# A text and image-prompt attention kernel: first maxima's remainder in PSUM, loads moved ahead, a score chunk ahead of the ip products

## What is computed

```python
q = heads(x @ W_q); k_t = heads(text @ W_k); v_t = heads(text @ W_v)
probs_t = softmax(q k_t^T * 0.25)                 # 112 x 371 per head
text_out = probs_t v_t
k_ip, v_ip = heads(ip @ W_k_ip), heads(ip @ W_v_ip)
qsem = l2norm(probs_t text)                       # 112 x 512 per head
sem = qsem l2norm(ip)^T                           # 112 x 4
probs_ip = softmax(q k_ip^T * 0.25 + 0.5 * sem) * mask
out = (text_out + probs_ip v_ip) @ W_out + b_out + x
```

## Time and profile before

| | |
|---|---|
| median of 3 runs | 394.98 us (394.34, 394.98, 399.27) |
| the profiled execution's own time | 399.06 us, span 396.9 us, 9414 instructions |
| PE (TensorE products) | 381.2 us busy, 96% of the span, x3596 |
| VectorE, ScalarE, GpSimd | 221.2, 206.1, 208.2 us busy |
| chain that ended last | PE 77%, DVE 7%, DMA 6%, ACT 3%, POOL 3%, issue 2% |
| DMA | 37.87 MB in 29328 packets, mean 95 GB/s |
| granted TensorE clock | mean 0.993 of full |

### The profile page before, as it was taken

How to read it: one execution, slowest core, us unless ns; L and a number is a source line. 1 busy time by engine, 2 the same in 40 slices (tenths; PEclk the granted TensorE clock), 3 DMA queues, 4 the chain that set the end, 5 groups by cost and what they waited for, 6 DMA issues and landing times.

```text
span 396.9 us, 9414 instructions
## 1 busy us (share of the span) xinstructions
PE 381.2 (96%) x3596; PEld 319.6 (81%) x3596; DVE 221.2 (56%) x493; ACT 206.1 (52%) x483; POOL 208.2 (52%) x229
## 2 busy tenths in 40 slices
PE   8999996999999999999999999999999999999984
PEld 5658896877888888888989888888888888887773
DVE  0798482476367634665466545664466546644434
ACT  1533132665746564645457464656455466458722
POOL 7010280184527962586428652796258532944972
PEclk9999999899999999999999999999999999999998
DMA  8869989248204802273207620580207310001010
GB/s 268 264 158 222 166 214 181 46 154 155 72 0 155 151 13 58 79 163 66 85 7 196 102 67 19 154 151 13 75 0 161 66 41 3 2 9 34 2 31 15
DMA packets 29328, 37.87 MB, mean 95 GB/s; under 512 B 14346, under 2 KB 26619, under 8 KB 28603
## 3 DMA queue, kind: packets, MB, share of 16 engines
q1 hardware_dynamic: 28388, 36.22, 38.9%
q10 hardware_dynamic: 896, 1.07, 0.9%
HBM read 28.36 MB, written 8.81 MB: 94 GB/s over the span
## 4 chain that ended last, share of the span: by engine, by line
PE 77%; DVE 7%; DMA 6%; ACT 3%; POOL 3%; issue 2%; SPq 1%; ACTq 0%; DVEq 0%; POOLq 0%
PE PR L1000 38%; PE Y L1000 24%; PE O L1000 8%; PE P L1000 6%; DMA et<-ctxT 4%; DVE mx L889 2%; DMA qst<-ma 2%; POOL pb L598 1%; ACT big L750 1%; PE PR L1173 1%; POOL t L625 1%; ACT eh L683 1%; PE PR L1110 1%; DVE kst L841 0%; DVE kst L843 0%
## 5 line engine op out<-in xcount | busy, mean ns | idle before, releaser
L598 POOL TENSOR_TENSOR pb<-pb 128x448 f32<-128x448 f32 x78 | 89.1, 1143 | 102.5 <-DVE pb L911 97.0
L889 DVE TENSOR_REDUCE mx<-PR 112x1 f32<-112x371 f32 x160 | 82.2, 536 | 78.4 <-PE PR L1000 78.0
L1000 PE MATMUL Y<-er,Gh 128*128 128x448 f32 x240 | 95.1, 396 | 1.5 <-ACT er L754 1.3
L911 DVE TENSOR_TENSOR pb<-big,Y 128x448 f32<-128x448 f32 x120 | 72.6, 620 | 36.9 <-PE Y L1000 35.3
L1000 PE MATMUL Y<-er,Gl 128*128 128x448 f32 x240 | 87.2, 363 | 0.0
L750 ACT ACTIVATE big<-P 128x448 f32<-128x448 f32 x120 | 65.1, 542 | 25.5 <-PE P L1000 25.2
L754 ACT ACTIVATE er<-big 128x448 fp32r<-128x448 f32 x120 | 69.4, 578 | 3.8
L1000 PEld LDWEIGHTS Y<-er,Gh 128*128 128x128 f32 x240 | 45.1, 188 | 12.5 <-DVE pb L911 8.2
L1000 PE MATMUL PR<-kst,qst 96*112 96x371 bf16 x160 | 50.4, 328 | 0.6 <-DVE mx L889 0.5
L1000 PEld LDWEIGHTS Y<-er,Gl 128*128 128x128 f32 x240 | 45.2, 188 | 2.2
L1000 PE MATMUL P<-qst,kst 99*128 99x112 bf16 x480 | 41.9, 213 | 3.8 <-DMA qst<-ma 3.7
(11 more groups left out here) (177 smaller groups left out, 668.4 us busy)
## 6 DMA issues: line engine op xcount, KB each, us to landing
et<-ctxT SPq DMA_DIRECT2D x8, 752.0 KB, 4.3
kst<-kd SPq DMA_DIRECT2D x7, 720.0 KB, 7.3
kd<-ks SPq DMA_DIRECT2D x16, 288.0 KB, 2.8
qst<-qd SPq DMA_DIRECT2D x48, 70.0 KB, 2.3
kst<-kd SPq DMA_DIRECT2D x7, 480.0 KB, 9.8
kst<-kd SPq DMA_DIRECT2D x9, 240.0 KB, 9.2
qd<-kst SPq DMA_DIRECT2D x4, 336.0 KB, 5.9
vx<-xr SPq DMA_DIRECT2D x8, 140.0 KB, 2.6
```

The costliest lines, as they stand in the source:

```text
L598: pool.tensor_tensor(total, total, (pz, pm)[j], ALU.add).then_inc(s_S, 1)
L889: dve.tensor_reduce(mx[b % 2][:, h:h + 1], bank[0:S, 0:T], AX.X, ALU.max).then_inc(s_free[seq[u] % NR], 1)
L911: dve.tensor_tensor((pz, pm, pa[g % 2])[j], eb[g % 3][:, 448 * j:448 * j + 448], Y[y % 2][:, 0:448], ALU.mult).then_inc(s_P, 1)
L1000: return pe.matmul(o, st, mv, start=start, stop=stop, **kw)
```

## The change

Five edits. The remainder of the maxima's split, `mr`, is no longer a tile in SBUF but lies in a free part of the transpose's own PSUM bank (columns 128 to 239), so the last operation reads one operand from PSUM, waits for the one before it (`link`), and it, not the third, frees the bank. `load_e(1)` goes ahead of the kd writes of batch 0. `load_q(1)` goes ahead of the wait for the kd writes of batch 1 and of the k(1) load. The halves of context 1's split go between G(0,0), G(0,1) and G(0,2) instead of ahead of all three. And the word lists: in batch 0 one maximum moves from the fourth round to the third and one ahead of that round's gram products, in batches 1 to 6 the next group's first score chunk goes ahead of `cT`, and in the last batch's second round `pw` goes behind the gram products.

```diff
-          "p E g2 g1 pT g0 cT S0 S1 v o S2")
+          "p E g2 g1 pT g0 S0 cT S1 v o S2")
 EARLY = ("m S1- m S2- K1 S0 m g m S1 m S2 K2 m",
          "S0 m g m S1 m S2 v m m wo C",
-         "S0 m g m S1 m v S2 m V1",
-         "Kr S0 m g m m S1 m m v mT S2 GV",
+         "S0 m g m S1 m v S2 m V1 m",
+         "Kr S0 m g m S1 m m v mT S2 GV",
          "E g S0 v S1 S2")
-LATE = "p g2 g1 pT g0 cT S0 S1 v S2 o"
+LATE = "p g2 g1 pT g0 S0 cT S1 v S2 o"
-        "S0 r0 g2 pw S1 g1 g0 S2 v",
+        "S0 r0 g2 S1 g1 g0 pw S2 v",
...
-    order += [("K", 0, c) for c in range(3)] + [("Kr", 0), ("w", 1)] + qs[1] + [("kip", c) for c in range(3)] + [("vip",)] + split(1)
-    order += [("G", 0, i) for i in range(3)] + [("K", 1, c) for c in range(3)] + [("Kr", 1)]
+    order += [("K", 0, c) for c in range(3)] + [("Kr", 0), ("w", 1)] + qs[1] + [("kip", c) for c in range(3)] + [("vip",)]
+    order += [("G", 0, 0)] + split(1)[:2] + [("G", 0, 1)] + split(1)[2:] + [("G", 0, 2)] + [("K", 1, c) for c in range(3)] + [("Kr", 1)]
...
                 if u[0] == "K" and u[1] == 0:
                     c = u[2]
+                    if c == 0:
+                        load_e(1)
                     sp.wait_ge(s_k0s, c + 1)
...
-                    else:
-                        load_e(1)
...
                         load_q(0)
+                    if b == 1:
+                        q_written(sp)
+                        load_q(1)
                     sp.wait_ge(s_kw, written(b + 1))
...
-                    if b == 1:
-                        q_written(sp)
...
-                    if b == 1:
-                        load_q(1)
...
-                    p = bank[0:H, 0:S]
+                    p, mr = bank[0:H, 0:S], bank[0:H, 128:128 + S]
                     link(dve.tensor_scalar(ma[:, 0, :], p, -1.0, None, ALU.mult))
                     dve.scalar_tensor_tensor(ma[:, 1, :], p, -1.0, ma[:, 0, :], ALU.mult, ALU.subtract)
-                    dve.scalar_tensor_tensor(mr[:, :], p, -1.0, ma[:, 0, :], ALU.mult, ALU.subtract).then_inc(s_free[seq[u] % NR], 1)
+                    link(dve.scalar_tensor_tensor(mr, p, -1.0, ma[:, 0, :], ALU.mult, ALU.subtract))
+                    dve.tensor_tensor(ma[:, 2, :], mr, ma[:, 1, :], ALU.subtract).then_inc(s_free[seq[u] % NR], 1)
                     freed(dve, seq[u])
-                    dve.tensor_tensor(ma[:, 2, :], mr[:, :], ma[:, 1, :], ALU.subtract).then_inc(s_ms, 1)
+                    dve.sem_inc(s_ms, 1)
```

More of the change, by code:

```diff
@@ L225, in build @@
         ma = sb("ma", [H, 3, S], bf16)
-        mr = sb("mr", [H, S])
         OT = [sb(f"OT{i}", [128, NG, S]) for i in range(2)]
```

## The result

The changed kernel takes 394.02 us (median of 22 runs, 392.97 to 396.79), the kernel before 395.93 us beside it (22 runs, 394.34 to 400.69): ratio 0.9948, 95% interval 0.9929 to 0.9968, a gain of 1.9 us. The time lies inside the range (389.0 to 394.3) and 2.6 us above the point.

The account below looks back on a forecast made before the run. TensorE was taken to bound the kernel from 75 to about 360 us, with one large hole at the prologue's end. Terms 5.1 + 0.45 + 0.4 - 0.3 = 5.65 us, 3.6 taken from the 394.98 median: 391.4, range 389.0 to 394.3.

Parts of the forecast that it names:

- The step from the profiled execution to the median: Whole kernel: median 4.1 us below the profiled execution, so 1.55 to 5.65 left to gain; middle 3.6 taken.
- (a): Prologue, split of the maxima: remainder in PSUM cuts the slow last operation, `ma` ready 1.1 us sooner; bounds 0 and 1.15.
- (b): Prologue, SyncE's queue: q(1) issued in a DMA pause ahead of k(1), out of `ma`'s way; 2 us, bounds 0 and 2.3.
- (c): Prologue loads: context 1 ahead of the first `kd` writes brings k(1) 1.5 us sooner; bounds 0 and 2.
- (d): Prologue, K(1,0): G(0,0) ahead of the context's split frees its bank in time; 0.3 us, bounds 0 and 0.44.
- Start and clock: End of the prologue: first score chunk 3.8 us sooner, and 1.3 us from a clock that doesn't fall; together 5.1.
- (e): Batch 0: a maximum one round earlier removes a wait before the transpose; 0.45 us, bounds 0 and 0.5.
- (f): Six batches: S0 ahead of cT fills TensorE's wait, 0.1 us each; net 0.4 us, bounds -0.3 and 0.7.
- (g): Last batch: the power behind the sums turns TensorE's wait into a later one; cost 0.3 us, bounds -0.5 and 0.5.
- The stall isn't in ordinary runs: Rival, prologue: (a) to (c) shorten what was short, 0.85 us left; 394.1 us, chance 0.17.
- `ma` still waits in the queue: Rival, prologue: k(1) not sooner, `ma` lands near 67 and the clock still falls; 393.2 us, chance 0.22.
- The slower one: Rival, first maximum: context 1 delays the `kd`(0) writes and k(0), so TensorE waits; 396.7 us, chance 0.06.

Follow-up runs that it names:

- aa_before: The kernel before, unchanged, measured again: median 396.65 us, 0.8 below the kernel before in its group; its profiled execution took 395.74 us.
- ma_act: The kernel before with the three `ma` writes of batch 0 issued by ScalarE instead of SyncE: 6.2 us slower than before, six runs.
- no_a: The changed kernel with the remainder of the maxima back in SBUF: 394.62 us, 2.1 below the kernel before.
- the profiled pair: The profiled executions of the kernel before and of the changed kernel: 399.06 against 395.17 us.
- only_b: The kernel before with only q(1) loaded ahead of k(1): 396.65 us, 1.6 below the kernel before.
- only_a: The kernel before with only the remainder of the maxima in PSUM: 397.85 us, 0.4 below the kernel before.
- only_c: The kernel before with only context 1 loaded ahead of the kd writes of batch 0: 396.54 us, 1.7 below the kernel before.
- only_d: The kernel before with only G(0,0) ahead of the split of context 1: 399.14 us, 0.9 above the kernel before.
- no_c: The changed kernel with context 1 back behind the kd writes of batch 0: 395.32 us, 1.4 below the kernel before.
- no_b: The changed kernel with q(1) back behind k(1): 396.42 us, 0.3 below the kernel before.
- after_again: The changed kernel, unchanged, measured again: 394.81 us, 2.4 below the kernel before.
- before_again: The kernel before, unchanged, measured once more: 396.81 us, 0.4 below the kernel before; its profiled execution took 399.6 us.
- rest_efg: The kernel before with the word-list edits alone: 397.16 us, 0.3 below the kernel before; its profiled execution took 402.34 us.
- early_again: The changed kernel with the last batch's power in its old place and each `ma` write issued when its piece is ready: 393.91 us, 3.3 below before.

## Why the prediction was off, point by point

- **The step from the profiled execution to the median** failed: "I take the middle, 3.6". It treated the 4.1 us between the profiled execution and the median as one quantity of which half might be gained. Executions are of two kinds, and the median of the first measurement is of the short one: in aa_before, which stands for it, wait 0.53 us and full clock. The three times shown (394.34, 394.98, 399.27) already had two near 395 and one like the profiled 399.06. Read so, the long wait and its clock drop of the earlier trace rows had to be left out of the sum for a median almost whole. The prediction had that case at the end of its own scale ("the median has 1.55 left to gain"), and the runs gained 1.9. Of 2.6 us of error 1.7 is this; the other 0.95 is that the median of 22 runs of before is 395.93, not 394.98.
- **(a)** The duration came out (0.263 us in the median of all eight batches). The 1.42 us stand in nine traces that keep `mr` in SBUF, and end 0.12 to 0.13 us behind `El` in each; in the ten with `mr` in PSUM the operation takes 0.26 with `El` running beside it. One more trace tells it from the other side: in ma_act's execution at the low clock TensorE's transpose came so late that `El` (84.05, 3.50 us) was over, and the unchanged operation with both inputs in SBUF took 0.263 us in batch 0. `ma` is issued 1.42 us behind the transpose instead of 2.51: 1.1 sooner, as forecast. The rule of the Trainium skill (SBUF — State Buffer, the section on the ports), that such an operation waits for GpSimd's whole instruction, agrees with all of these. In time (a) showed no worth. Where TensorE waited for `ma`, k(1)'s end and not readiness set the landing; in no_a, where k(1) ended early (5.0 us behind the transpose), the late issue rather set it (`ma`'s last packet ended 1.3 us behind k(1)'s, in after 0.3), and TensorE had other work until then.
- **(b)** Forecast 2 us (0 to 2.3), measured 2.4 between the profiled pair (from k(1)'s last packet to the chunk 4.3, then 1.9), 2.1 to 3.4 over all traces. This edit by itself leaves no long runs (only_b: none of 12 above 398 us, where only_a has 5, only_c 3 and only_d 7). Of 121 runs with it in all kernels one is above 398, in no_c. The other edits together may do the same: no_b has none of 12, at a median 1.8 above no_a's. The ring-order rule of the Trainium skill (DMA: Bandwidth & Descriptors, queues, rings and completion order) isn't contradicted: wherever all of k(1) stood ahead of `ma` on SyncE's queue, the last `ma` packet ended behind k(1)'s last (64.70 against 64.43 us in after). The pause wasn't the one named: q(1)'s packets ran from 51.4 to 54.2 us, ahead of 54 to 56, in a time in which before had shares of 0.97 and 0.73 and after has 0.63 and 0.53.
- **(c)** Forecast k(1) 1.5 us sooner. Against the first q product k(1)'s last packet ends 1.14 us sooner in the pair, but from one execution to the next it moves by more than that (55.6 and 58.0 us behind it in aa_before and before, 56.8 and 57.8 in after and after_again), so that the size of (c) isn't shown. What the working missed is its second effect: context 1 itself comes in time, and no trace with (c) has a wait at K(1,0).
- **(d)** Forecast 0.3, bounds 0 to 0.44. In the pair 0.24; in ordinary executions the wait that it removes was 0 to 1.71 us, with a clock drop at the upper end. The bound had come from one trace. (c) alone and (d) alone each remove it.
- **Start and clock.** Forecast 3.8 + 1.3 for the pair; measured, start set aside, 3.55 and 1.3.
- **(e)** Forecast 0.45, measured 0.33 to 0.39. The wait for a bank is gone, and the transpose, reached sooner, now waits 0.59 us for the last maximum:

```profile
93.01 0.26 PE L1109 MATMUL PR<-ident,mx 112*20 112x112 f32 x1 [0.59 <-DVE mx L887]
```

- **(f)** Forecast 0.4 as 0.1 at six places, bounds -0.3 and 0.7; measured 0.54 to 0.84, nearly all of it at one place that the working didn't have. From batch 1's to batch 6's transpose the profiled kernels take 212.78 and 212.77: S0 ahead of cT is worth nothing there, the 0.1 that it gains is given back within the round. But behind batch 5's fifth round, where only two maxima stand between the chunks and the next gram products (the first of batch 6), TensorE waited for ScalarE's copy of the exponential. Before, then after:

```profile
320.34 0.48 PE L1000 MATMUL PR<-kst,qst 96*112 96x371 bf16 x2
321.25 0.44 PE L1000 MATMUL Y<-er,Gh 128*128 128x448 f32 x1 [0.43 <-ACT er L754]
```
```profile
315.73 0.48 PE L999 MATMUL PR<-kst,qst 96*112 96x371 bf16 x2
315.92 0.49 PE L999 MATMUL Y<-er,Gh 128*128 128x448 f32 x1
```

From maximum to gram product it is 0.91 us and then 0.19. The likely reason, not tested alone, is that the chunk, moved 1.5 us up, starts ScalarE's chain sooner. A like wait in the last batch's second round (0.58 us) stayed.
- **(g)** Forecast a cost of 0.3, measured 0.23 in the pair and 0.4 against the traces that have (f) and the power in its old place. GpSimd idles 0.34 us before the sums, then does the power, and TensorE's wait has moved to a gram product. GpSimd, then TensorE, after:

```profile
361.66 2.44 POOL L596 TENSOR_TENSOR pb<-pb 128x448 f32<-128x448 f32 x2 [0.34 <-DVE pb L910]
364.06 3.54 POOL L623 TENSOR_TENSOR t<-ssq,halfm 112x20 f32<-112x20 f32 x1
```
```profile
369.69 0.47 PE L999 MATMUL Y<-er,Gh 128*128 128x448 f32 x1 [0.67 <-DVE pb L910]
```

- **The rivals.** "The stall isn't in ordinary runs", 394.1 us at 0.17, is nearest to what happened, though its time is right partly by luck: it gained 0.85 from 394.98, the kernel gained 1.9 from 395.93, the rest being (f) and K(1,0). "`ma` still waits in the queue" is true as a mechanism (k(1) sets the landing), but `ma`'s packets ended at 64.7 us and the clock didn't fall. The slower one didn't occur: the first maximum waits in none of the traces with (c).

What stays open is why the DMA work between 44 and 54 us goes faster in some executions than in others, and so what makes an execution long. The `kd` writes of batch 1 land 1.6 to 1.7 us behind the end of their last issue in some traces (aa_before, only_a, only_d) and 3.7 to 4.0 in those with the longest waits (before, before_again, rest_efg), with these transfers in the same order; only_c, with 2.3 and a wait of 2.70, doesn't fit between them.

## What to carry to other kernels

Before a sum made from one profiled execution is set against a median, ask which kind of execution was profiled. Here the wait on a DMA near full engines was 0.5 us in one execution of the kernel before and 3.9 in another, the times showed it as runs about 1% above the rest, and such a wait belongs in the sum only with the share of runs that have it; the steady terms, however small, carry the median. And in front of a late transfer look at what stands ahead of it in its queue before making its data ready sooner.

## What the runs showed of the hardware

- TensorE's clock around a wait. In all traces at full clock together, waits of 0.24 to 1.38 us left the granted clock at its upper level (2.4 GHz); with those of 1.71, 1.78, 1.94, 2.70, 3.32, 3.67, 3.78 and 3.90 us it fell to the lower (1.2 GHz), and 12 products of q took 6.47 us instead of 4.78 (rest_efg). At the first chunk that adds 1.3 to 2.2 us to the wait: from there to the gram 5.1 to 6.0 us instead of 3.8.
- The first input load varies too: TensorE's first q product starts at 6.5 to 8.5 us, and in two of the traces (rest_efg and early_again) late enough for the slow products. It is in kernels with and without the change.
- One execution (ma_act) ran at a clock of 0.56 from end to end, 605 us; its kernel's other seven runs were at 401.5 to 405.6.
